# Attention and mixture-of-experts layer on one core: x normalised block by block inside the pair loop, loads put behind the first stack, row maxima padded to 128 columns, GpSimd subtractions in four pieces

## What is computed

```
x = x + attn(layernorm(x))      # per block of 512 tokens, 16 heads of 64
x = x + ffn(layernorm(x))       # 64 experts, 8 of them per token, and a shared one

# attn, on h = layernorm(x)
q, k, v = h @ Wq + bq, h @ Wk + bk, h @ Wv + bv
ctx = softmax(q k^T / 8) v
y = h + ctx @ Wo + bo
return (y - mean(y)) * rsqrt(var(y) + 1e-3) * gamma + beta
```

## Time and profile before

| | us |
|---|---|
| runs, median of 3 | 1416.04 (1414.08 to 1416.6) |
| the profiled execution, its own time | 1419.42 |
| its span | 1417.7 |
| PE busy | 1359.0 (96%) |
| DVE busy | 1086.9 (77%) |
| POOL busy | 910.1 (64%) |
| ACT busy | 865.9 (61%) |
| first matmul of the first pair's scores | 50.8 |
| step of the pair loop in the steady state | 11.61 |

### The profile page before, as it was taken

One profiled execution on the slowest core, in us unless ns is written; L12 is line 12 of the kernel. 1 busy time (PEld: TensorE's weight loads), 2 busy tenths in 40 slices (PEclk: granted clock), 3 DMA queues, 4 the chain that ended last, 5 costly groups with the idle time before them and its releaser, 6 DMA issues.

```text
span 1417.7 us, 35701 instructions
## 1 busy us (share of the span) xinstructions
PE 1359.0 (96%) x12985; PEld 771.3 (54%) x12985; DVE 1086.9 (77%) x1925; ACT 865.9 (61%) x1560; POOL 910.1 (64%) x682
## 2 busy tenths in 40 slices
PE   3799999999999999999998899999999999999998
PEld 1366666666666666666656544444444444444443
DVE  5777777777777778777878768777777877786865
ACT  3566666666666666666666555656555555656554
POOL 3576777777776777777777655647464655656554
PEclk9999999999999999999999899999999999999999
DMA  7233332333333333333332000000000000000000
GB/s 182 56 76 83 77 84 71 87 76 78 79 74 80 74 80 74 80 74 80 82 80 52 9 0 9 8 1 16 1 16 0 15 0 15 0 10 5 1 8 8
DMA packets 84823, 67.38 MB, mean 48 GB/s; under 512 B 27792, under 2 KB 75216, under 8 KB 84688
## 3 DMA queue, kind: packets, MB, share of 16 engines
q1 hardware_dynamic: 84688, 65.52, 18.7%
HBM read 13.05 MB, written 2.10 MB: 11 GB/s over the span
## 4 chain that ended last, share of the span: by engine, by line
PE 74%; DVE 9%; issue 9%; POOL 4%; ACT 2%; SPq 2%; DVEq 0%; DMA 0%; POOLq 0%; ACTq 0%
PE bank L1019 72%; POOL arena L518 3%; DVE arena L977 2%; PE bank L1206 2%; DVE arena L922 1%; POOL arena L483 1%; DVE arena L983 1%; ACT arena L664 1%; DVE arena L779 0%; SPq L334 0%; SPq L339 0%; DVE arena L757 0%; DVE arena L842 0%; SPq L333 0%; DVE arena L942 0%
## 5 line engine op out<-in xcount | busy, mean ns | idle before, releaser
L1019 PE MATMUL bank<-arena 128*128 128x512 f16 (+5 forms) x12600 | 1328.6, 266 | 44.2 <-DVE arena L922 8.5
L1019 PEld LDWEIGHTS bank<-arena 128*128 128x128 f16 (+3 forms) x12600 | 726.6, 98 | 612.5 <-issue 41.4
L483 POOL TENSOR_TENSOR arena<-arena 128x1024 f16<-128x1024 f32 x256 | 484.8, 1894 | 224.9 <-ACT arena L626 221.1
L518 POOL TENSOR_TENSOR arena<-arena 128x512 f16<-128x512 f32 x264 | 306.7, 1167 | 223.7 <-ACT arena L669 221.8
L922 DVE TENSOR_REDUCE arena<-bank 128x2 f32<-128x1024 f32 x256 | 312.2, 1220 | 58.1 <-PE bank L1019 54.6
L626 ACT ACTIVATE arena<-bank 128x512 f32<-128x512 f32 x512 | 276.8, 595 | 82.3 <-PE bank L1019 82.3
L977 DVE TENSOR_TENSOR arena<-arena,bank 128x512 f32<-128x512 f32 x256 | 175.4, 685 | 113.3 <-ACT arena L664 67.9
L669 ACT ACTIVATE arena<-arena 128x512 f16<-128x512 f32 x264 | 165.5, 627 | 154.2 <-DVE arena L983 152.5
L983 DVE TENSOR_TENSOR arena<-arena,bank 128x512 f32<-128x512 f32 x256 | 176.1, 688 | 28.2 <-DVE arena L977 3.6
L664 ACT ACTIVATE arena<-bank 128x512 f32<-128x512 f32 x264 | 155.1, 588 | 63.6 <-PE bank L1019 58.1
L615 ACT ACTIVATE arena<-bank,arena 128x512 f16<-128x512 f32 x128 | 88.0, 688 | 155.6 <-PE bank L1019 155.6
(11 more groups left out here) (106 smaller groups left out, 428.4 us busy)
## 6 DMA issues: line engine op xcount, KB each, us to landing
arena<-arena SPq DMA_DIRECT2D x384, 128.0 KB, 2.4
arena<-in_L_attn_x SPq DMA_DIRECT2D x9, 256.0 KB, 2.8
arena<-in_L_ffn_Wg SPq DMA_DIRECT2D x32, 64.0 KB, 2.1
arena<-in_L_ffn_Wu SPq DMA_DIRECT2D x32, 64.0 KB, 2.2
arena<-in_L_ffn_Wd SPq DMA_DIRECT2D x32, 64.0 KB, 2.2
out<-arena SPq DMA_DIRECT2D x8, 256.0 KB, 2.3
arena<-in_L_attn_Wq SPq DMA_DIRECT2D x1, 512.0 KB, 4.1
arena<-in_L_attn_Wk SPq DMA_DIRECT2D x1, 512.0 KB, 5.2
```

Of the source, the lines that this page charges most:

```text
L483: pool.tensor_tensor(num_lo[:, u % 2, s, :, :], num[:, u % 2, s, :, :], num_hi[:, u % 2, s, :, :, 1], ALU.subtract).then_inc(lo_pool, 1)
L518: pool.tensor_tensor(hid_lo[:, r, :], hid[:, r, :], hid_hi[:, r, :], ALU.subtract).then_inc(hid_lo_done, 1)
L1019: return nc.tensor.matmul(out_, lhsT, rhs, start=start, stop=stop, skip_group_check=True)
```

## The change

1. **x block by block.** Only block 0 is normalised and transposed ahead of the pairs. Blocks 1 to 7 are normalised by ACT (scale and bias per tile of tokens, the bias made by one small DVE step) at the end of step n + n//2, and turned at the end of step n + n//2 + 1, into `ps_proj`, between the split of v and the next projection of q. POOL and DVE normalise nothing of them. The steps -3 to 11 are now written out (`FIRST` is 12).
2. **Loads behind the first stack.** SP issues Wv, Wo, the vectors, the router weights and the shared expert after the six copies of the first stack. Waits are cut to fit: `in_vo` for Wv and Wo, `Q_READY`, `V_READY` and `ROUTER_READY` for single results. The splits of Wv and Wo stand in steps -1, the bias row in step 0. Pair 0's maxima go to three different banks (`max_bank`), and k of pair 0 to a bank of its own (`proj_bank`).
3. **Row maxima padded.** `negmax` has 128 columns per tile, zero but for columns 64 and 65, and the four small matmuls have a full 128-column weight and write all 128 partitions.
4. **GpSimd in four pieces.** The subtraction of 128 x 1024 becomes four of 128 x 256; the first two wait for the first head's exponential alone. The subtraction of 128 x 512 in the expert stage becomes four of 128 x 128.

```
-FIRST, LOOP_END = 4, 52
+FIRST, LOOP_END = 12, 52
...
-        negmax = f16(take(2 * QT)).rearrange("p (r t h) -> p r t h", r=2, t=QT)
+        negmax = f16(take(2 * QT * P // 2)).rearrange("p (r t c) -> p r t c", r=2, t=QT)
...
+        def max_bank(pair, q):
+            return (bank[2], bank[0], bank[1], bank[2])[q] if isinstance(pair, int) and pair == 0 else bank[2]
+        def proj_bank(t, which):
+            return ps8[1] if isinstance(t, int) and (t, which) == (0, 1) else ps_proj
...
+                if isinstance(p, int) and p == -3:
+                    load_rest()
...
-            pool.wait_ge(a_rstd, 2)
-            for n in range(NORM_POOL, B):
-                for t in range(n * QT, (n + 1) * QT):
-                    last = pool.tensor_scalar(xn[:, t, :], xn[:, t, :], stat[:, 0, t:t + 1], stat[:, 1, t:t + 1],
-                                              ALU.subtract, ALU.mult)
-                last.then_inc(a_norm_pool, 1)
...
-                    pool.wait_ge(exp_done, 8 * p + 2 * s + 2)
-                    if s == 0:
-                        wait(pool, ctx_ps, 2 * (p - 2) + 2)
-                    pool.tensor_tensor(num_lo[:, u % 2, s, :, :], num[:, u % 2, s, :, :],
-                                       num_hi[:, u % 2, s, :, :, 1], ALU.subtract).then_inc(lo_pool, 1)
+                    for h in range(2):
+                        pool.wait_ge(exp_done, 8 * p + 2 * s + h + 1)
+                        if s == 0 and h == 0:
+                            wait(pool, ctx_ps, 2 * (p - 2) + 2)
+                        for q in (slice(0, S // 2), slice(S // 2, S)):
+                            last = pool.tensor_tensor(num_lo[:, u % 2, s, h, q], num[:, u % 2, s, h, q],
+                                                      num_hi[:, u % 2, s, h, q, 1], ALU.subtract)
+                    last.then_inc(lo_pool, 1)
...
-                pool.tensor_tensor(hid_lo[:, r, :], hid[:, r, :], hid_hi[:, r, :],
-                                   ALU.subtract).then_inc(hid_lo_done, 1)
+                for q in range(QT):
+                    at = slice(q * P, (q + 1) * P)
+                    last = pool.tensor_tensor(hid_lo[:, r, at], hid[:, r, at], hid_hi[:, r, at], ALU.subtract)
+                last.then_inc(hid_lo_done, 1)
...
+                if (p, s) in NORM_AT:
+                    act.wait_ge(a_shift, 1)
+                    n, tiles = NORM_AT[p, s]
+                    for t in tiles:
+                        at = n * QT + t
+                        last = nc.scalar.activation(xn[:, at, :], xn[:, at, :], ACT.Identity,
+                                                    bias=stat[:, 7, at:at + 1], scale=stat[:, 1, at:at + 1])
+                    if t == QT - 1:
+                        last.then_inc(a_norm, 1)
...
-                            last = mm(ps_turn[K:K + 2, k * P:(k + 1) * P], negmax[:, (u + 1) % 2, k, :], ident16, True, True)
+                            last = mm(ps_turn[:, k * P:(k + 1) * P], negmax[:, (u + 1) % 2, k, :], ident16, True, True)
...
-                        if isinstance(p, int) and p == 0 and s == 0:
-                            pe.wait_ge(tr_a_lo, B)
...
+                            if (p - 1, 3) in TURN_AT:
+                                pe.wait_ge(tr_a_lo, TURN_AT[p - 1, 3] + 1)
...
-NORM_AT = {(-2, 3): (1, 2), (-1, 0): (3, 4), (-1, 1): (5,)}
-NORM_POOL = 6
-TURN_AT = {(-1, 0): (1,), (-1, 1): (2, 3), (-1, 2): (4, 5), (-1, 3): (6, 7)}
+TURN_AT = {(n + n // 2 + 1, 3): n for n in range(1, B)}
+NORM_AT = {(n + n // 2, 3): (n, range(QT)) for n in range(1, B)}
```

More of the change, by code:

```diff
@@ L182, in layer @@
         ps_ctx = ps8[3]
-        ps_max2 = bank[2]
         ps_proj = ps8[6]
@@ L194, in layer @@
         in_qk = sem("in_qk")
+        in_vo = sem("in_vo")
         in_rest = sem("in_rest")
@@ L614, in hi @@
                     bias = (bq8, bk_c)[which]
-                    nc.scalar.activation(flat[:, (u + 3) % 2, (ZQH, ZKH)[which], :], ps_proj, ACT.Identity,
+                    nc.scalar.activation(flat[:, (u + 3) % 2, (ZQH, ZKH)[which], :], proj_bank(t, which), ACT.Identity,
                                          bias=bias[:, n:n + 1]).then_inc(qk_hi, 1)
@@ L1124, in query_tile @@
                         pe.wait_ge(stacked[up % 2], 96 * (half + 1))
-                    wait(pe, max_done, 4 * pair + q)
+                    wait(pe, max_done, 4 * pair + q if pair > 0 else q - 2)
                     for h in range(2):
                         st = stack[:, up % 4, h, :, :]
-                        last = mm(ps_max2[:, h * S:(h + 1) * S], st[:, Q1, q * P:(q + 1) * P], st[:, K1, :], True, True)
+                        last = mm(max_bank(pair, q)[:, h * S:(h + 1) * S], st[:, Q1, q * P:(q + 1) * P], st[:, K1, :], True, True)
                     last.then_inc(max_scores, 1)
@@ L1152, in run @@
                             pe.wait_ge(v_lo_done, p)
+                        if p == 1 and s == 0:
+                            pe.wait_ge(dve_step, A_DONE)
                         for k in range(QT):
@@ L1207, in run @@
                         last.then_inc(ctx_t, 1)
-                    if isinstance(p, int) and p < 0:
+                    if isinstance(p, int) and p < FIRST:
                         rest_of_a(p, s)
```

142 lines of the change are left out of this document (77 added, 65 removed).

## The result

| | before | after |
|---|---|---|
| runs, median | 1416.32 (1414.08 to 1417.28, 4 runs) | 1396.43 (1394.63 to 1397.18, 4 runs) |
| the profiled execution, its own time | 1419.42 | 1397.18 |
| its span | 1417.7 | 1395.5 |

The ratio is 0.986, with a 95% interval of 0.9843 to 0.9877. The medians lie 19.9 us apart and the two profiled executions 22.2: the profiled one of before was 3.1 above its median, the one of after 0.8.

A forecast was written before the change was run, and what follows sets the result against it. PE, busy 96% of 1417.7 us, was taken as the bound through its own order of work. Terms -13.5 + 3.5 - 11.0 + 0.4 = -20.6 took 1419.42 to 1398.8, and 3.4 less for the median gave 1395.5; range 1388 to 1408.

The forecast's parts named there:

- Case A: Whole kernel: the forecast itself comes true, own range 1390 to 1401 us; chance 0.62.
- Part 1, the start: Before pair 0: scores start at 35.2 us instead of 50.8, less 2.1 given back; net -13.5 us, bounds -16 and -8.
- the second stack goes out from 25.3: SP's queue at the start: second stack issued from 25.3 to 28.5 us, behind eleven loads, landing at 31 to 32.
- The 0.48 us apiece: SP's queue between the stacks: each of eleven loads holds SP 0.48 us, 5.3 us in all.
- Given back in pair 0: Pair 0: bias row in PE's way, DVE's backlog and PE's low clock together cost 2.1 us.
- Part 2, the blocks: Seven blocks in the pairs: transposes cost PE 0.44 us each, plus 0.06 a block; +3.5 us, bounds 3.1 and 8.
- Part 3, the padding: Row-maxima matmuls in the pairs: full-width weights save 0.19 us a step; -11.0 us, bounds 0 and -12.
- rival B: Row-maxima matmuls: padding does nothing, the gaps being a semaphore wait and not the width; 1406.5 us, chance 0.10.
- Part 4, the pieces: POOL subtractions: pieces of 590 ns in the pairs, 0 us; of 409 ns in the expert stage, +0.4 us at the end.
- who waits: Pairs: PE's context matmuls need the last low part at 318.0, POOL ends at 317.90; slack 0.1 us.
- C: Start or blocks give back more: second stack late behind the loads, each block stalling 0.7 us; 1403.5 us, chance 0.16.
- D: POOL becomes the bound: PE stalls from pieces of 0.63 us on; 1413 us, or 1532 at 804 ns; chance 0.12.

The follow-up runs named there:

- experiment 9: Changed kernel with V's bias fetched with Q's and K's, only Wv and Wo between the stacks, seven loads behind the second, bias row in pair 0: 1397.25 us.
- experiment 7: Changed kernel with the late weight loads (Wv, Wo, router, shared expert) issued ahead of the first stack again: 1397.67 us.
- experiment 2: Kernel before with the padded row maxima alone, plus the buffer and fill of zeros they need: 1408.57 us.
- experiments 5 and 6: Changed kernel with a row-maxima weight of the 64 upper columns (1408.65 us), and of the 66 lower columns (1397.46 us), instead of 128.
- experiment 3: Changed kernel with the pairs' POOL subtraction in one piece of 128x1024 again, after both exponentials: 1399.33 us.
- experiments 11, 12: Changed kernel with the expert stage's POOL subtraction in one piece of 128x512 (1398.73 us), and in two pieces of 256 (1396.96 us).

## Why the prediction held, and where it did not

The forecast was 1395.5 with a range of 1388 to 1408, and 1396.43 came. Case A happened. The sum is closer than its terms.

- **Part 1, the start (-13.5).** -13.9 + 2.3 = -11.6. The first stack was within 0.3 us. The step that failed is "the second stack goes out from 25.3": it went at 27.39, since the eleven loads took 7.5 us on SP's queue and not 5.3; pair 0's first score matmul came at 36.7, 1.5 later than foretold. The 0.48 us apiece were too low from the start: behind the one of 4.54 us the other ten had held SP for 8.7 us before, two of them (V's bias and gamma) for 1.46 and 3.07. That a queue was full, as the prediction says of the 4.54, no run shows. "Given back in pair 0" was right in size, 2.3 us, and it holds both things I named: the bias row, 2.0 (experiment 9), and the low clock, which lasts 5.0 us into pair 0 and 3.4 us in it before. How the 2.3 divide was not measured. But the part of the change that moves the loads earns at most some 0.9 us at pair 0 and nothing to be seen at pair 1 (experiment 7). I had seen that the loads delay the second stack, but not that this takes back the whole gain. What remains of the part, the block-wise normalisation with the banks and splits of its own, was not taken apart further.
- **Part 2, the blocks (+3.5).** A step with a block takes 11.88 or 11.89 us, one without 11.44: 0.44 for each of seven, 3.1. No block stalls; the 0.06 I had added are not there.
- **Part 3, the padding (-11.0).** Undone by itself it costs 9.3 us by the times, 0.172 a step where I read 0.188 out of narrow windows. Put in by itself it earns 0.131 a step (experiment 2), 7.5 us over 57; the other 0.04 need the pieces. The gaps are gone: 300.41 to 300.62 is the plain step, and the fourth row maximum is followed by the next matmul at the usual 0.056. What the missing 0.016 is stays open. As I took it, and against rival B, it is the form of the weight and not the wait. That its narrowness does it is not shown: by experiments 5 and 6 and the float32 group it can as well be the place of the output, partitions from 64 on.
- **Part 4, the pieces (0 and +0.4).** This term had the wrong sign. The durations were nearly right (615 and 436 ns for 590 and 409), the check "who waits" was asked for POOL's end alone. It missed two things. First, part 3 lets PE come earlier, so the slack of 0.1 us of the earlier trace rows would have been gone without the division: 2.4 us (experiment 3), a gain that neither part has alone. Second, DVE waits for POOL's running instruction, and PE for DVE: some 2 us in the expert stage (experiments 11, 12). It could have been read before: the trace had the 1.26 us of L873 beside means of 0.42 for the same form. The Trainium skill, "SBUF — State Buffer", section on SBUF's two separate sides, has the rule: VectorE and GpSimd take a shared pair of ports exclusively for a whole instruction where VectorE has two operands in SBUF. The trace agrees, with 0.28 us behind the end of POOL's instruction each time.
- **The rivals.** C's condition, a second stack late behind the loads, came in part (landed at 33.5 instead of 31 to 32) and its blocks' stalls did not. B and D fell: with pieces of 615 ns D's point of 0.63 was near, and from 85 us on PE shows no wait for POOL; the two waits in pairs 1 and 2 (1.3 us in all) were there before too.

By what was measured the terms are -11.6, +3.1, -9.9 for padding and pieces together in the pairs (7.5 and 2.4), and -2.0 for the pieces in the experts: -20.4, against -20.6 foretold and 19.9 between the medians. The start was put 1.9 us too high and the pairs 1.1, the blocks 0.4 too dear, and the experts' pieces 2.4 too low. The right total owes something to these cancelling. The 2.2 us of pair 63 itself stand in none of these terms. It takes 11.5 to 12.0 us in the three profiles with an undivided subtraction in the pairs (before, experiments 2 and 3) and 9.2 to 10.8 in the other eleven, so the pieces are likely part of it. How much of it is in the medians is not known: the profiled execution of before was 3.1 us above its own.

## What to carry to other kernels

Ask of a transfer that is moved back in a queue what it is now ahead of: here both positions cost the same transfer time before pair 0. Where a small 16-bit matmul in a full-size stream has a gap on either side that no other engine ends, try it with a full-width weight that begins at partition 0; here 66 or 128 columns from there cost nothing, since the load is hidden. And where VectorE's operations with both operands in SBUF stand beside long GpSimd ones, look at the spread of their durations, not the mean: dividing the GpSimd instruction shortens the longest wait, and two pieces may do as well as four. A wait found to have 0.1 us of slack must be costed again together with every part that makes its reader faster.

## What the runs showed of the hardware that I had not expected

- A VectorE operation of 0.42 us with both operands in SBUF takes 1.26 us when a GpSimd subtraction of 1.17 us is under way, 0.78 with pieces of 256 elements, 0.53 with pieces of 128. One with an operand in PSUM in the same stretch keeps its 0.67 to 0.69.
- A group of four 16-bit matmuls with a weight of 64 columns for partitions 64 to 127 costs 0.20 us more than one with 66 columns for partitions 0 to 65, and slightly more than one of two columns (0.17). Four float32 transposes with 64 columns for partitions 0 to 63 lose nothing.
- TensorE's granted clock in pair 0 was 0.78 on the average in after, which had worked in short pieces from 21.7 on and got the full clock at 42.2, and 1.00 in experiment 7, which had been idle for 6.8 us, worked without a pause from 28.2 to 33.1 and got the full clock at 33.2. Pair 1 started at 49.3 in both.
- The time from the last score to the end varies by 2.6 us between profiles of kernels with divided subtractions there (612.2 to 614.8), more than one of the terms argued over. Only the mean over the profiles, and TensorE's idle times behind L977 and its like, show the 2.0 us.
